# Attention gather in two column groups of TensorE with a spreading product, first keys fetched earlier

## The reference

```python
h = layernorm(x) * (1 + ca) + sa
q, k, v = heads(h @ Wq + bq), heads(h @ Wk + bk), heads(h @ Wv + bv)
scores = q @ k.T / 4
sparsity = scores.max(-1) - scores.mean(-1)
top_idx = top_k(sparsity, 307)                 # per batch and head
q_sel = take_along_axis(q, top_idx)            # 307 of 2048 queries
out_sel = softmax(q_sel @ k.T / 4) @ v         # over all 2048 keys
x = x + ga * (zeros.at[top_idx].set(out_sel) @ Wo + bo)
x = x + gb * soft_moe(layernorm(x) * (1 + cb) + sb)   # 8 experts of 128 slots
```

## Time and profile before

| | |
|---|---|
| median of three runs | 1648.62 us |
| profiled execution, its own time | 1640.96 us |
| span of the profiled execution | 1638.9 us |
| TensorE matmul busy | 1501.4 us (92%) |
| TensorE weight load busy | 837.0 us (51%) |
| VectorE busy | 1218.9 us (74%) |
| ScalarE busy | 1041.9 us (64%) |
| GpSimd busy | 267.0 us (16%) |
| attend(0), start of the first gather to start of the last scores | 455.3 to 592.4 us |
| attend(1), the same | 952.8 to 1086.9 us |

### The profile page before, as it was taken

How to read it: one execution, slowest core, us unless ns; L and a number is a source line. 1 busy time by engine, 2 the same in 40 slices (tenths; PEclk the granted TensorE clock), 3 DMA queues, 4 the chain that set the end, 5 groups by cost and what they waited for, 6 DMA issues and landing times.

```text
span 1638.9 us, 28513 instructions
## 1 busy us (share of the span) xinstructions
PE 1501.4 (92%) x8674; PEld 837.0 (51%) x8674; DVE 1218.9 (74%) x2910; ACT 1041.9 (64%) x1404; POOL 267.0 (16%) x317
## 2 busy tenths in 40 slices
PE   7989999998779999999998989989999999989999
PEld 3532222223345532222222745544788986479988
DVE  6689999999866759999999887856756443675511
ACT  4588888887546678888887547763343473333464
POOL 2430000004413362000000213341111000111100
PEclk9999999999989999999999999999999999999999
DMA  5751111131522201111112211120134302014410
GB/s 187 245 154 39 51 45 39 39 97 39 165 63 68 64 19 39 50 47 39 39 40 89 67 32 50 53 64 24 39 123 162 102 29 77 0 33 156 163 48 32
DMA packets 93457, 119.38 MB, mean 73 GB/s; under 512 B 22862, under 2 KB 78766, under 8 KB 92860
## 3 DMA queue, kind: packets, MB, share of 16 engines
q1 hardware_dynamic: 90300, 117.66, 23.5%
q0 software_dynamic: 3072, 0.66, 0.4%
HBM read 93.46 MB, written 24.79 MB: 72 GB/s over the span
## 4 chain that ended last, share of the span: by engine, by line
PE 46%; DVE 33%; issue 13%; DMA 3%; ACT 3%; POOL 1%; SPq 0%; DVEq 0%; ACTq 0%; POOLq 0%
DVE work_area L1239 25%; PE psum L2045 7%; PE psum L2109 6%; PE psum L1890 5%; PE psum L1913 5%; PE psum L1988 4%; PE psum L1904 4%; PE psum L2056 3%; DVE big_area L1239 2%; PE psum L2065 2%; DMA work_area<-heads_out 2%; PE psum L2099 2%; PE psum L1746 1%; PE psum L1721 1%; ACT big_area L919 1%
## 5 line engine op out<-in xcount | busy, mean ns | idle before, releaser
L1239 DVE CUSTOM_DVE_ANT_0 work_area<-psum,work_area 128x1024 f32<-128x1024 f32 x512 | 589.3, 1220 | 9.5 <-PE psum L1782 5.5
L849 ACT ACTIVATE work_area<-psum 128x1024 f32<-128x1024 f32 x512 | 510.4, 1026 | 78.1 <-DVE big_area L1239 29.1
L1782 PE MATMUL psum<-work_area 96*128 96x512 bf16 x1024 | 310.7, 385 | 48.1 <-DVE big_area L1239 7.5
L1772 PE MATMUL psum<-work_area 96*128 96x512 bf16 x1024 | 306.0, 381 | 7.7 <-ACT work_area L849 2.3
L1782 PEld LDWEIGHTS psum<-work_area 96*128 96x128 bf16 x1024 | 63.8, 97 | 266.9 <-DVE big_area L1239 250.8
L867 ACT ACTIVATE work_area<-psum 128x614 f32<-128x614 f32 x192 | 124.0, 681 | 87.7 <-PE psum L1904 87.5
L1772 PEld LDWEIGHTS psum<-work_area 96*128 96x128 bf16 x1024 | 89.1, 98 | 153.3 <-ACT work_area L849 58.6
L703 POOL DMA_INDIRECT heads_out<-work_area x96 | 98.0, 1021 | 190.9 <-DVE work_area L1394 169.8
L1988 PE MATMUL psum<-slots_T,work_area 128*128 128x512 f32 x256 | 117.5, 603 | 0.0
L2045 PE MATMUL psum<-work_area,xn 128*128 128x128 f32 x1024 | 117.2, 275 | 0.0
L2109 PE MATMUL psum<-expert_out,work_area 128*128 128x256 f32 x512 | 115.6, 379 | 1.1 <-ACT work_area L984 1.1
(11 more groups left out here) (255 smaller groups left out, 2046.4 us busy)
## 6 DMA issues: line engine op xcount, KB each, us to landing
work_area<-in_L_ffn_w_dram SPq DMA_DIRECT2D x32, 1024.0 KB, 5.5
work_area<-k_parts SPq DMA_DIRECT2D x192, 64.2 KB, 2.1
work_area<-q_parts SPq DMA_DIRECT2D x192, 64.0 KB, 2.2
k_parts<-work_area SPq DMA_DIRECT2D x24, 384.0 KB, 4.0
q_parts<-work_area SPq DMA_DIRECT2D x16, 384.0 KB, 2.5
big_area<-q_parts SPq DMA_DIRECT2D x16, 384.0 KB, 5.3
work_area<-k_parts SPq DMA_DIRECT2D x32, 192.0 KB
x_res<-in_L_attn_x_dram SPq DMA_DIRECT2D x8, 512.0 KB, 6.7
```

The lines of the kernel that those rows point to most:

```text
L849: s.activation(SC[:, t % 4], PS[:, 2 * (n % 2):2 * (n % 2) + 2].rearrange("p a n -> p (a n)"), ACT.Relu).then_inc(relu_done, 1)
L1239: v.tensor_tensor_reduce(SC[:, t % 4], PS[:, 4 + 2 * (t % 2):6 + 2 * (t % 2)].rearrange("p a n -> p (a n)"), SC[:, t % 4], 1.0, -3.0e38, A ...
L1772: last = mm(PS[:, 2 * (n % 2) + k], QS1[par][0:TERMS, t * P:(t + 1) * P], KS[par][0:TERMS, k * 512:(k + 1) * 512], start=True, stop=True)
L1782: last = mm(PS[:, 4 + 2 * (t % 2) + k], QS1[par][0:TERMS, t * P:(t + 1) * P], KS[par][0:TERMS, K1 + k * 512:K1 + (k + 1) * 512], start=Tru ...
```

## The change

The query parts are gathered once each: `SK` has 64 columns a tile (48 of parts, 3 of maxima, 2 of the index, 11 of zeros that GpSimd writes in `pads`), and even and odd tiles go to rows 0 to 63 and rows 64 to 127 of PSUM bank 4, in two column groups of the array. ScalarE copies the 128 x 307 sums to `GQ` (bfloat16), and one more matmul, `spread` (L1920 of the new kernel), with a zero-one matrix `spread_rows` adds the two halves and repeats the parts, which gives the 101 rows as before. The gather has two pieces of 8 tiles in place of three of 5, 6 and 5. GpSimd makes `spread_rows` at the program's start. SyncE issues the ones and the keys of heads 0 and 1 of batch 0 ahead of all stores of batch 1's units, and in `attention_keys(0)` it waits for the gather of head h before it issues the terms of batch 1.

```diff
         a.at = 4 * HALF
-        SK = a.take([2, NT, TERMS + 6], BF16)
+        SK = a.take([2, NT, HALF_ROWS], BF16)
+        GQ = a.take([UP], BF16)
         PX.append(a.take([2, UP]))
         OR = a.take([CH, DH + 1])
...
+                            sp.wait_ge(gathered, h + 3)
                             key_term(1, (h - 2) // 6 * DH, (h - 2) // 6, k)
                             query_term(1, (h - 2) // 6 * DH, (h - 2) // 6, k)
...
                 queries_to_sbuf(0, g)
+            key_ones(0)
+            for par in range(2):
+                first_keys(0, par)
             for u in range(NU):
                 parts_to_dram(1, u)
                 if u == share(G + 1)[-1]:
                     queries_to_sbuf(0, 3)
-                if u == 8:
-                    key_ones(0)
-                if u == 12:
-                    for par in range(2):
-                        first_keys(0, par)
             attention_keys(0)
             other_heads(1)
...
+            for half in range(2):
+                for at, part in enumerate((0, 0, 0, 1, 1, 2)):
+                    cols = spread_rows[:, at * DH:(at + 1) * DH]
+                    g.affine_select(out=cols, in_=cols, compare_op=ALU.not_equal, fill=1.0, base=-(half * HALF_ROWS + part * DH), pattern=[[-1, DH]], channel_multiplier=1)
+                cols = spread_rows[:, TERMS:TERMS + 5]
+                last = g.affine_select(out=cols, in_=cols, compare_op=ALU.not_equal, fill=1.0, base=-(half * HALF_ROWS + PARTS), pattern=[[-1, 5]], channel_multiplier=1)
+                last.then_inc(pstep, 1)
+                pool.wait_ge(pstep, ps.next())
             for q in range(ROUNDS):
...
                 pool.wait_ge(sp_ready, 2 * b + 2)
+                g.memset(SK[:, :, :, PARTS + 5:].rearrange("p a t c -> p (a t) c"), 0.0)
                 g.memset(OS[:, U:], 1.0).then_inc(pads_ready, 1)
 
...
 
+                def take_gathered(i, n):
+
+                    act.wait_ge(gathered, b * H + i * 2 + (n + 3))
+                    s.activation(GQ[:, 0:U], PS[:, 4, 0:U], ACT.Identity).then_inc(gq_ready, 1)
+
                 def take_queries(i, par, n):
 
...
                 take_queries(0, 0, 0)
 
                 def act_head(i, par, more):
-                    for k in range(7):
+                    late = i == 0 and par == 0
+                    for k in range(8):
                         exps(i, par, (k,))
+                        if more and k == (5 if late else 3):
+                            take_gathered(i, par + 1)
+                        if more and k == (6 if late else 5):
+                            take_queries(i, 1 - par, par + 1)
                         if b == 0 and i == 0 and par == 0 and 1 <= k <= 3:
                             second_part(1, NU - 4 + k)
-                    if more:
-                        take_queries(i, 1 - par, par + 1)
-                    exps(i, par, range(7, 8))
 
                 for h in range(H):
...
+                    v.tensor_copy(SK[:, par, :, PARTS + 3:PARTS + 5], qidx[:])
                 dve.wait_ge(prefix_ready, b + 1)
...
-                for at, r in enumerate((0, 0, 0, 1, 1, 2)):
-                    v.tensor_copy(SK[:, par, :, at * DH:(at + 1) * DH], QN[:, :, r, bass.ds(hd, DH)])
-                v.tensor_copy(SK[:, par, :, TERMS:TERMS + 3], NM[:, :, bass.ds(h, 1)].rearrange("p t o r -> p t (o r)")).then_inc(sk_ready, 1)
+                v.tensor_copy(SK[:, par, :, 0:PARTS].rearrange("p t (r d) -> p t r d", r=3), QN[:, :, :, bass.ds(hd, DH)])
+                v.tensor_copy(SK[:, par, :, PARTS:PARTS + 3], NM[:, :, bass.ds(h, 1)].rearrange("p t o r -> p t (o r)")).then_inc(sk_ready, 1)
 
 
...
                                 pe.wait_ge(oh_ready, b * H + 1)
-                        last = mm(PS[0:TERMS + 5, 4, 0:U], SK[:, n % 2, t, 0:TERMS + 5], OH[:, n % 2, t, 0:U], start=(t == 0), stop=(t == NT - 1), skip_group_check=True)
+                        at = t % 2 * HALF_ROWS
+                        last = mm(PS[at:at + HALF_ROWS, 4, 0:U], SK[:, n % 2, t], OH[:, n % 2, t, 0:U], start=(t < 2), stop=(t >= NT - 2), skip_group_check=True)
                     if NT - 1 in tiles:
                         last.then_inc(gathered, 1)
+
+                def spread(i, n):
+
+                    pe.wait_ge(gq_ready, b * H + i * 2 + (n + 1))
+                    mm(PS[0:TERMS + 5, 4, 0:U], spread_rows[:, 0:TERMS + 5], GQ[:, 0:U], start=True, stop=True).then_inc(spread_ready, 1)
 
                 def scores(i, n, k):
...
                 def pe_head(i, n, first, later):
-                    CUTS = (0, 0, NT // 2, NT) if first else (0, 5, 11, NT)
                     for k4 in range(3):
                         scores(i, n, 2 * k4 + 2)
                         scores(i, n, 2 * k4 + 3)
                         values(i, n, k4)
-                        if k4 < 2 and later > 0:
-                            gather(i, n + 1, range(CUTS[k4 + 1], CUTS[k4 + 2]))
+                        if later > 0 and k4 < (2 if first else 1):
+                            gather(i, n + 1, range(k4 * (NT // 2) if first else NT // 2, (k4 + 1) * (NT // 2) if first else NT))
+                        if later > 0 and k4 == (2 if first else 1):
+                            spread(i, n + 1)
                         if k4 == 2:
                             if first and b == 1:
...
                     if later > 1:
-                        gather(i, n + 2, range(0, 5))
-
+                        gather(i, n + 2, range(NT // 2))
+
+                pe.wait_ge(pads_ready, b + 1)
                 gather(0, 0, range(NT), True)
+                spread(0, 0)
                 scores(0, 0, 0)
                 if b == 0:
                     pe.wait_ge(resid_ready, B * NU)
```

More of the change, by code:

```diff
@@ L95, in adaln_block @@
     UP = U + 1
+    HALF_ROWS = 64
+    PARTS = 3 * DH
     CH = (U + P - 1) // P
@@ L164, in adaln_block @@
         hcol = sb("hcol", [P, H])
+        spread_rows = sb("spread_rows", [P, TERMS + 6], BF16)
         shiftB = sb("rank_shift", [P, 2], BF16)
@@ L333, in adaln_block @@
         oh_ready, gathered, idx_ready, idx_used = sem("oh_ready"), sem("gathered"), sem("idx_ready"), sem("idx_used")
+        gq_ready, spread_ready = sem("gathered_copied"), sem("gathered_spread")
         qs_ready, s_ready, p_ready, p_used = sem("qs_ready"), sem("s_ready"), sem("p_ready"), sem("p_used")
@@ L624, in _ @@
             pool.wait_ge(pstep, ps.next())
+            g.memset(spread_rows[:], 0.0).then_inc(pstep, 1)
+            pool.wait_ge(pstep, ps.next())
[6 more added lines that the diff above has]
+                last.then_inc(pstep, 1)
+                pool.wait_ge(pstep, ps.next())
             for q in range(ROUNDS):
@@ L854, in attend @@
             def attend(b):
+                def take_gathered(i, n):
+                    act.wait_ge(gathered, b * H + i * 2 + (n + 3))
+                    s.activation(GQ[:, 0:U], PS[:, 4, 0:U], ACT.Identity).then_inc(gq_ready, 1)
                 def take_queries(i, par, n):
-                    act.wait_ge(gathered, b * H + i * 2 + (n + 3))
+                    act.wait_ge(spread_ready, b * H + i * 2 + (n + 1))
                     s.activation(QS[0:TERMS + 5, par, 0:U], PS[0:TERMS + 5, 4, 0:U], ACT.Identity).then_inc(qs_ready, 1)
@@ L869, in attend @@
                 s.activation(warm[:], onesF[:, 0:1], ACT.Exp)
+                take_gathered(0, 0)
                 take_queries(0, 0, 0)
                 def act_head(i, par, more):
-                    for k in range(7):
+                    late = i == 0 and par == 0
+                    for k in range(8):
                         exps(i, par, (k,))
+                        if more and k == (5 if late else 3):
+                            take_gathered(i, par + 1)
+                        if more and k == (6 if late else 5):
+                            take_queries(i, 1 - par, par + 1)
                         if b == 0 and i == 0 and par == 0 and 1 <= k <= 3:
                             second_part(1, NU - 4 + k)
-                    if more:
-                        take_queries(i, 1 - par, par + 1)
-                    exps(i, par, range(7, 8))
                 for h in range(H):
```

1 line of the change is left out of this document (removed).

## The result

| | median of 12 (lowest to highest) | profiled execution, its span |
|---|---|---|
| before | 1650.55 us (1646.44 to 1654.69) | 1640.96, 1638.9 |
| after | 1659.46 us (1655.19 to 1662.14) | 1655.92, 1654.1 |

The ratio is 1.0049 (95%: 1.0037 to 1.006): the changed kernel is 0.5% slower. 1631.8 us was forecast, with 0.84 for faster.

What follows compares the result with a forecast made beforehand. TensorE was taken as the bound, with the key fetch nearly a second one. Terms -5.0 - 5.9 + 0 - 3.9 - 2.0 = -16.8 us, put on the median of 1648.62, gave 1631.8 us; range 1624 to 1644.

Steps and rivals of the forecast that it cites:

- heads 2 to 15 of batch 0: Attention heads, batch 0: shorter gather, and fetch from 9.6 to 9.2 us, save 0.46 us each over 13, -5.9 us.
- heads 2 to 15 of batch 1: Attention heads, batch 1: with a key fetch of 8.8 us, 0.38 us saved a head over 13, -5.0 us.
- the fetch's wait on the chain: Ahead of scores 0: two key buffers make the fetch nearly a second bound, hidden by under 1 us in batch 1.
- Gather: Per head on TensorE: two pieces of 0.65 us and a 0.13 spread replace 2.23 us, saving 0.80; a pair costs one pitch.
- Hand-over: ScalarE's extra copy per head delays exp 5: 0.2 to 0.25 us wait at scores 7, TensorE's head about 7.4 us.
- the worst case of 7.7: Upper bound of TensorE's head in us, if the spread waits for its copy too; the lower bound was 7.1.
- From the trace to the median: Whole kernel: -16.8 us, summed against the profiled 1640.96, put on the median of 1648.62, 7.66 higher, giving 1631.8.
- Start of attend(0): Before batch 0's heads: earlier stores -2.5, builds -0.8, first gather -2.0, copy, hand-over and spread +1.4; sum -3.9 us.
- Head 2 of batch 0: Its keys queue behind the last stores; what heads 0 and 1 save only lengthens its stall of 3.08 us: 0.
- Start of attend(1): Before batch 1's heads: three builds at -0.4 each and a shorter gather of head 2, -2.0 us (bounds 0 and -3).
- no overlap of the column groups: Rival, gather: a pair of 64-column matmuls takes 0.26 us, TensorE's head 8.4; +5.3, 1654 us; chance 0.09.
- a hand-over that stalls more: Rival: TensorE's head 7.7 us; batch 1 -3.0, batch 0 -4.0, with the starts -12.9, 1636 us; chance 0.11.

Runs made afterwards that it cites:

- e13: The changed kernel unaltered, timed again beside the kernel before on a chip with signals on time: 1618.16 us against 1641.15, ratio 0.9857.
- e12: Changed kernel with one-hots written through a 7 by 44 view, which was lost, so the changed kernel once more: 1619.31 us, ratio 0.9849 to the kernel before.
- e2: The kernel before with only the ones and first keys issued ahead of batch 1's parts: 1650.96 us against 1656.18, ratio 0.9977.
- e5: Changed kernel's order and hand-over, but the old gather products of 101 columns in the whole array: 1633.79 us, kernel before 1640.97.
- e6: Changed kernel without the 90 scatters of the heads' rows, attention's output unwritten: 1612.65 us, kernel before 1640.97.
- e17: Changed kernel without the scatters, as e6, on another chip: 1618.53 us against 1639.49 for the kernel before, ratio 0.9882.
- e18: Changed kernel without the scatters, as e17, on another chip: 1619.85 us against 1640.71 for the kernel before, ratio 0.9875.

## Why the prediction was wrong

Where signals are on time its sum comes out, -15.9 us in the traces for -16.8, but partly by luck: single terms are off by 1.5 to 3 us in both directions. e13's trace against the one before, step by step:

| step | forecast | e13 |
|---|---|---|
| first scores of batch 0 | -3.9 | 459.77 to 458.92, -0.9 (e12: -2.4) |
| from there to head 2 | 0 | -1.0 |
| heads 2 to 15 of batch 0 | 8.21 to 7.75, -5.9 | 8.12 to 7.67, -5.9 |
| first scores to head 2, batch 1 | -2.0 | -4.3 |
| heads 2 to 15 of batch 1 | 7.93 to 7.55, -5.0 | 7.83 to 7.56, -3.5 |
| the rest | 0 | -0.3 |
| sum | -16.8 | 1638.9 to 1623.1: -15.9 |

The medians on that chip differ by 23.0; this execution of the changed kernel was the longest of four, 1624.89 us where the median is 1618.16. Its stretches and the fetch's wait on the chain, which is what the prediction said the change would run into:

```profile
483.00:592.00 109.00, 101.63 (x959) 41.85 (x956) 65.02 (x278) 77.47 (x137) 42.58 (x42) 0.99 0.22 61
984.00:1080.00 96.00, 88.25 (x846) 36.93 (x846) 71.20 (x286) 74.63 (x151) 40.32 (x40) 0.99 0.17 49
```

```profile
1003.17 0.26 PE psum L1920
1003.43 0.62 PE psum L1932 x4
...
1005.42 0.77 issue
```

- *Gather.* Pairs start 2 to 4 ns apart and 0.13 after each other, a piece is 0.64 to 0.65 us, loads of 64 columns take 109 ns. Right, on both kinds of chip.
- *Hand-over.* Forecast 0.2 to 0.25 us and a TensorE head of 7.4; with signals on time it is 7.25, a wait of some 0.1. **This is the step that failed in the measurement**: where signals are late, most heads of batch 1 take 8.4 to 8.6 us and those of batch 0 9.4 to 10.6. The copy, the spread and exps 4 and 5 form a chain of four steps that starts at one late signal; I gave each signal the 0.33 us that the trace showed, where the first measurement has 0.6 to 2.6, and the worst case of 7.7 only asked whether the spread waits, not whether the signal is late.
- *The clock.* In batch 0, where a head takes 2.4 us more than 7.25 in the mean, the granted clock falls to half in six stretches, 0.85 in the mean; the prediction had no such term for the heads. In batch 1, with 1.3 us of waits a head, it stays at 1.00.
- *From the trace to the median.* I noted that the profiled execution was 7.66 us under the median, and put the difference on the median. That gap was the sign: on the chips without late signals the kernel before has medians of 1639.5 to 1642.6 us, with this execution's 1640.96 among them, and where e2 shows that the old attention has them its median is 1656.18. That the runs timed for the prediction had late signals is thus an inference; none of them has a trace. The size fits only roughly: e2's heads against those of the trace before give (0.76 + 0.39) x 13 = 15.0 us, but its whole span is 6.8 us longer (1645.7 for 1638.9), since its start is 2.9 shorter and other parts 5.3.
- *The balance.* On time, the change gives -23.0 us. The changed kernel's two traces, of the first measurement and of e13, differ by 1654.1 - 1623.1 = 31.0 us. Heads 2 to 15 are (2.01 + 0.74) x 13 = 35.8 longer, and the rest goes the other way, above all head 2 of batch 0 (7.25 us for 10.88). Between medians of different chips, late signals cost the changed kernel 1659.46 - 1618.16 = 41.3 us and the kernel before 1650.55 - 1641.15 = 9.4; that these and the -23.0 add up to the measured +8.9 is so by construction and checks nothing.
- *Start of attend(0).* -3.9 was too much: -0.9 and -2.4 (e12) in two runs. The steps named were about right. From VectorE's first one-hot of head 0 to the first gather it is 11.35 us in e13 instead of 14.16, the gather takes 2.27 instead of 3.95, and the hand-over at half clock takes back 1.0, together -3.5. But that first one-hot starts 2.6 us later (443.77 for 441.14). Of this 1.4 us come from the program's start, where the prediction put GpSimd's constants at 0 because GpSimd is idle there. Before, and in e13:

```profile
6.22 1.65 POOL L627 MEMSET bit_steps<- 128x1 int32 x48
9.16 0.17 DVE L1103 TENSOR_SCALAR rs_v<-mean_var 128x4 f32<-128x4 f32 x1
```

```profile
9.00 1.65 POOL L641 MEMSET bit_steps<- 128x1 int32 x48
9.14 1.53 DVE L1126 TENSOR_SCALAR rs_v<-mean_var 128x4 f32<-128x4 f32 x1
```

The 14 operations for `spread_rows` move GpSimd's 48 small writes to where VectorE has an operation of the first layer norm; it now takes 1.53 us instead of 0.17 and ends 0.02 us after them, and ScalarE and all that follows are 1.4 us later. In e5, which builds the matrix with one operation, the writes are over at 8.53 and VectorE's operation takes 0.17 again. The rest of e13's delay is a stretch at half clock, 0.57 in the mean of 389 to 393 us, where the traces of before and of e12 have 1.00.
- *Head 2 of batch 0.* Put at 0. The step from head 1 to it takes 12.71 us before and 7.25, 8.30 and 12.53 for one and the same kernel in e6, e17 and e18, all with signals on time. The time at which its keys are issued does not explain that: e17 has 465.46 and e18 465.36. So some 5 us of a single trace's span can come from this one wait, and no run shows why.
- *Start of attend(1).* Put at -2.0 with bounds of 0 and -3; e13 and e12 have -4.3 and -4.4. The wait of 1.52 us for the one-hots is gone; the rest was not followed further.

The rival that ended slower, no overlap of the column groups, was the wrong mechanism. None of the rivals had the signal's latency in it; the nearest, a hand-over that stalls more, allowed 0.3 us a head for a spread that waits, and still came out faster than before.

The kernel with the one-hots held has 0.987 and 0.9877 where signals are on time (the changed kernel: 0.9857, and 0.9849 as e12), and 0.990 where they are late (the changed kernel: 1.0049, perhaps on another such chip). The two were never run side by side on a chip with late signals, so that holding the one-hots helps there is likely, but not shown.

## What to carry to other kernels

Compare the profiled execution with the timed runs before the first sum. Here a gap of 0.5%, with every timed run above the profiled one, was the sign that the trace lacked something that the timed runs had, and a difference read from it could not be put on their median. A new dependency costs the latency of its signal as often as it stands in the program, so give each a bad case from other work that runs beside it, and place it where nothing is queued behind the waiting instruction. When several quite different edits all cure a fault, run the faulty kernel again beside them before believing any. And setup work on an idle engine is not free when it pushes that engine's next work beside another's: here 2.8 us of GpSimd's moved everything behind it by 1.4.

## What the runs showed of the hardware

- A copy that waits for TensorE's semaphore signal starts 0.33 or 0.34 us after the start of the matmul that gives it on five chips, in every head (0.50 to 0.51 at half clock). On two others, and where the change was first measured, it is 0.4 to 2.7 us in most heads, with TensorE's matmuls starting on time meanwhile. The kernel before takes 0.6 to 0.9% longer on them. Whether only the signals are late, or the results too, no run shows.
- The Trainium skill (SBUF — State Buffer, section Who interferes with whom) has the port pair of VectorE and GpSimd as the only contention among engines. On the five chips the traces agree: TensorE's signals are on time beside one-hots and scatters, and a stall between VectorE and GpSimd stands at the program's start, 1.53 us for 0.17; that it is of the ports is likely, not shown. On the two others, and in the first measurement, signals of TensorE arrive near the end of the other engines' work: in batch 1 0.15 to 0.18 us ahead of a scatter's end in the rows shown, in batch 0 at 527.58 and 537.99, 0.75 and 0.65 us behind a scatter's end. Whether that is a port, the semaphores or something else, no run here shows.
- Two 64-column products in two column groups take the time of one; one of 101 columns and one of 66 take 8.18 and 8.13 us a head, so the 35 columns between them are worth next to nothing.
